# A 2-D recurrent scan on one core: the last output stage on four quadrants, and two fetches of `seq` later in the queue

## The chip, the cores and the metric

The kernel runs on one core of a Trainium2 chip. The metric is device time in microseconds (us) of one execution, median of three runs. Names of the engines: PE multiplies matrices (PEld is its weight load), DVE and ACT work on vectors, POOL on vectors too, SP only issues transfers here. PSUM is the memory that PE writes (the `bank`s), SBUF the one with 128 lanes that all engines read; DMA engines move data between SBUF and the chip's DRAM.

## The reference

`x` is (8 images, 192 channels, 128, 128) in fp32. It is group-normed (32 groups), then scanned by one GRU of 64 states in four directions (along the rows and the columns, forward and backward, same weights), each scan's states are projected back to 192 channels, and the mean of the four is added to `x`:

```
def _scan_direction(x, Wi, bi, W_ih, W_hh, b_ih, b_hh, Wo, bo, transpose, reverse):
    xs = jnp.transpose(x, (0, 3, 2, 1)) if transpose else jnp.transpose(x, (0, 2, 3, 1))
    if reverse:
        xs = xs[:, :, ::-1, :]
    seq = xs.reshape(b * A, T, c) @ Wi.T + bi
    hs = _gru_scan(seq, W_ih, W_hh, b_ih, b_hh)      # r, z, n gates, 128 steps
    out = hs @ Wo.T + bo
    ...
return x + (right + down + left + up) / 4.0          # of the group-normed x
```

## The kernel before

Images go in pairs: lanes 0 to 63 hold one image's 64 values, lanes 64 to 127 (`HIGH`; the others are `LOW`) the other's. There are four pairs, `g` = 0 to 3. For a pair, `seq` (128 lanes x 16384 pixels) holds the projected input of the GRU and `hsum` the sum of the states of all directions. A pair's **scan** has 128 steps `t`; each step does two chains, `c` = 0 (rows) and 1 (columns), 256 positions each, both directions in one. So the four scans are 4 x 128 steps one after the other.

Beside the scan of pair `g` other work is woven into its steps, by tables that are computed at the top:

- the **next pair's input**: x of pair g + 1 comes in 32 tiles of 512 pixels (m = 0 to 31) through three slots `xp`, is projected by PE (`project_high`, `project_straight`, `project_crossed`), gets its bias on ACT into `stage`, and goes out to DRAM as `seq_next`, two tiles at a time (`store_seq`). `project_at` gives the step at which a tile's first matmuls run (71 + 7m // 4), `project_ends` the step of its last ones. `x_next_at` asks for a tile's x four steps before.
- **`seq` is refilled while the scan still reads it.** A scan reads pixels from both ends and turns at the middle, so squares of `seq` become free one after the other. `fetch_seq(g, k)` brings square k = 0, 1, 2 (2 MB, 2.4 MB, 1.3 MB) from `seq_next` to `seq`; before, at step `grown_at[k] + 4` = 99, 115, 123. It waits on SP until `seq_next`'s tiles of this square have landed (`stage_stored`). The borders follow by `fetch_border`.
- the **last pair's output**: 96 units (a third of a tile each) of pair g - 1 are multiplied by `Wo` on PE in quadrants of 64 x 64, `hsum` coming back from DRAM and x again into `xf`; these tiles already lie in the form "k c", 3 blocks of 64 channels on 64 lanes.

All of these transfers are issued by SP, in the order of one loop over the steps. SP takes one after the other: while it waits for a semaphore at one of them, nothing behind it is issued.

The last pair has no scan after it, so its output is the stage called **End** (`finish_last` on PE and DVE, `load_last` on SP, `store_last` on ACT): 32 tiles of 512 pixels, for each three banks of (128 lanes x 512). A tile of x, 0.786 MB, is loaded to one of 14 slots `xe`, `Wo`'s product is added to it in place, and it is stored from the same slot. Tile i >= 14 can be loaded only once tile i - 14 has been stored. Slots 0 to 13 are loaded in the last scan's steps, as their memory (`xp`, blocks of `seq`, `xf`) comes free. The banks are used in two sets of three, so PE starts tile i when DVE has finished tile i - 2. In the form before, blocks 0 and 1 of a slot hold channels 0 to 127 of image one and two, on 128 lanes, and block 2 the other 64 channels of both images:

```
def finish_last():                       # PE, before
    for k, wo in enumerate((wo_a, wo_b, wo_c)):
        for side in range(2):
            last = pe.matmul(natural(fin_ps[s][k][:, :], side), wo[:, :],
                             columns(hsum[:, :, rows_of(i), :], side), ...)
```

## Time and profile before

| | us |
|---|---|
| median of 3 runs | 2526.6 (2522.61 to 2531.65) |
| the profiled execution | 2523.95 |
| its span | 2522.2 |
| statistics and first projection, up to the first step | some 200 |
| four scans, up to 2406.6 | some 2200 |
| End, from 2406.6 | 115.6 |

| engine | busy us | share of the span |
|---|---|---|
| PE | 2199.8 | 87% |
| DVE | 2035.9 | 81% |
| ACT | 1621.5 | 64% |
| POOL | 1533.2 | 61% |

How to read it: the shares are of the whole span, and each stretch has a limit of its own. The granted clock of PE was 0.987 of full speed over the span. In the page's 40 slices the DMA engines are busy 9 tenths of the time at the start, in the later halves of the scans of pairs 0 to 2, and in the last two slices. Times in the rows are from the start of the span. The time from a transfer's issue to its landing is in the views too.

### The profile page before, as it was taken

Reading aid. Unit: us, or ns where it says so; the run is one execution under the profiler, and the core shown is the slowest. Engines: PE = TensorE matmul, PEld = TensorE weight load, DVE = VectorE, ACT = ScalarE, POOL = GpSimd, SP = SyncE. Lnnn points to the kernel's source line nnn. Section 1 sums busy time; section 2 is a strip of 40 time slices with the busy share of each in tenths; the row PEclk is TensorE's granted clock in tenths of the full one; section 3 lists DMA queues with packets and bytes.
Section 4 is the critical chain, followed back from the end, with each engine's and each line's share of the span. In section 5 each row is a group of like instructions: output and inputs, shape, how many; then the busy total and the mean of one; then the engine's idle time right before and its main releaser. Section 6 shows DMA issues by size and latency. Waiting matters only on the chain.

```text
span 2522.2 us, 80883 instructions
## 1 busy us (share of the span) xinstructions
PE 2199.8 (87%) x31528; PEld 1444.4 (57%) x31528; DVE 2035.9 (81%) x4883; ACT 1621.5 (64%) x3401; POOL 1533.2 (61%) x2114
## 2 busy tenths in 40 slices
PE   0679999899979999899979999899979999999995
PEld 0345555566546666566656666566656677555574
DVE  7229999777769999787879999888867777888874
ACT  0236666677758887676758788677657888666600
POOL 2016666667766666566766666667666677666610
PEclk9999999999999999999999999999999999999998
DMA  9983332347789997589999998589986655333699
GB/s 355 288 219 96 96 96 67 85 141 218 230 241 244 240 246 177 153 224 260 308 267 250 233 246 207 142 221 263 313 258 165 152 146 129 73 94 94 154 322 363
DMA packets 325723, 509.25 MB, mean 202 GB/s; under 512 B 24928, under 2 KB 140000, under 8 KB 325344
## 3 DMA queue, kind: packets, MB, share of 16 engines
q1 hardware_dynamic: 307296, 478.23, 69.0%
q10 hardware_dynamic: 18048, 25.85, 2.9%
q8 instruction: 252, 4.13, 0.7%
q14 instruction: 127, 1.04, 0.1%
HBM read 352.98 MB, written 151.01 MB: 200 GB/s over the span
## 4 chain that ended last, share of the span: by engine, by line
PE 34%; DVE 22%; ACT 22%; issue 11%; DMA 6%; POOL 3%; SPq 1%; ACTq 0%; POOLq 0%; DVEq 0%
PE bank L855 19%; DVE r L994 8%; ACT bank L663 8%; ACT r L655 7%; ACT z L659 7%; DVE h L1008 5%; DMA work<-x 4%; DVE bank L999 4%; PE bank L856 4%; PE bank L835 3%; DVE r L989 2%; PE bank L837 2%; PE bank L953 2%; POOL hsum L529 1%; DVE bn L1119 1%
## 5 line engine op out<-in xcount | busy, mean ns | idle before, releaser
L855 PE MATMUL bank<-h,wh 64*64 64x256 f32 x6144 | 1515.0, 384 | 121.2 <-DVE h L1008 120.6
L835 PE MATMUL bank<-seq,wx 64*64 64x256 f32 x6144 | 1551.3, 385 | 62.7 <-DMA seq<-seq_next 24.0
L837 PE MATMUL bank<-seq,wx 64*64 64x256 f32 x6144 | 1551.9, 385 | 0.0
L856 PE MATMUL bank<-h,wh 64*64 64x256 f32 x6144 | 1523.9, 386 | 0.3 <-issue 0.3
L537 POOL TENSOR_TENSOR v<-z,h 128x256 f32<-128x256 f32 x1024 | 746.9, 730 | 778.7 <-ACT z L659 777.6
L855 PEld LDWEIGHTS bank<-h,wh 64*64 64x64 f32 x6144 | 727.4, 132 | 483.6 <-PE bank L837 336.6
L835 PEld LDWEIGHTS bank<-seq,wx 64*64 64x64 f32 x6144 | 741.7, 132 | 355.9 <-DVE r L994 208.2
L545 POOL TENSOR_TENSOR hsum<-hsum,h 128x256 f32<-128x256 f32 x1024 | 752.0, 734 | 94.1 <-DVE h L1008 65.1
L837 PEld LDWEIGHTS bank<-seq,wx 64*64 64x64 f32 x6144 | 740.0, 132 | 16.7 <-issue 1.2
L856 PEld LDWEIGHTS bank<-h,wh 64*64 64x64 f32 x6144 | 730.3, 132 | 1.2 <-issue 0.7
L989 DVE SCALAR_TENSOR_TENSOR r<-bank,bhh,r 128x256 f32<-128x256 f32 x1024 | 491.0, 479 | 296.0 <-ACT r L655 242.3
L659 ACT ACTIVATE z<-bank,brz 128x256 f32<-128x256 f32 x1024 | 486.5, 475 | 313.0 <-PE bank L856 300.1
L655 ACT ACTIVATE r<-bank,brz 128x256 f32<-128x256 f32 x1024 | 486.6, 475 | 211.9 <-PE bank L856 200.9
L663 ACT ACTIVATE bank<-r,bih 128x256 f32<-128x256 f32 x1024 | 488.3, 477 | 85.8 <-DVE r L994 59.4
L999 DVE SCALAR_TENSOR_TENSOR bank<-z,bank 128x256 f32<-128x256 f32 x1024 | 434.2, 424 | 74.9 <-ACT bank L663 71.2
L994 DVE TENSOR_TENSOR r<-bank,r 128x256 f32<-128x256 f32 x1024 | 431.2, 421 | 17.6
L1008 DVE TENSOR_TENSOR h<-v,bank 128x256 f32<-128x256 f32 x1024 | 425.5, 416 | 22.3 <-POOL v L537 1.6
L981 DVE BATCH_NORM_STATS2 bn<-work 128x6 f32<-128x384 f32 x384 | 212.4, 553 | 4.0 <-DMA work<-x 4.0
L819 PE MATMUL bank<-work,wo_a 64*64 64x256 f32 x768 | 202.6, 381 | 1.3 <-issue 1.3
L803 PE MATMUL bank<-work,ident 64*64 64x256 f32 x756 | 203.0, 389 | 0.0
L821 PE MATMUL bank<-work,wo_b 64*64 64x256 f32 x768 | 202.2, 381 | 0.0
L801 PE MATMUL bank<-work,ident 64*64 64x256 f32 x756 | 197.5, 381 | 0.8 <-DMA work<-x 0.8
(95 smaller groups left out, 2446.6 us busy)
## 6 DMA issues: line engine op xcount, KB each, us to landing
work<-x SPq DMA_DIRECT2D x384, 384.0 KB, 6.2
out<-work SPq DMA_DIRECT2D x192, 384.0 KB, 4.7
work<-x SPq DMA_DIRECT2D x143, 512.0 KB, 7.1
work<-x SPq DMA_DIRECT2D x286, 128.0 KB, 7.1
work<-x SPq DMA_DIRECT2D x32, 768.0 KB, 6.5
seq_next<-work SPq DMA_DIRECT2D x48, 512.0 KB, 6.3
work<-hsum_last SPq DMA_DIRECT2D x48, 512.0 KB, 6.5
seq<-x SPq DMA_DIRECT2D x17, 512.0 KB, 7.6
```

The costliest lines, as they stand in the source:

```text
L537: pool.tensor_tensor(v[:, c, :], z[:, c, :], h[:, c, (t + 1) % 2, :], ALU.mult).then_inc(v_ready[c], 1)
L545: pool.tensor_tensor(px, px, as_pair(h[:, c, t % 2, :], c), ALU.add).then_inc(h_added[c], 1)
L655: act.activation(r[:, c, :], rx_ps[c][:, 0:N2], ACT.Sigmoid, bias=brz[:, 0:1]).then_inc(r_ready[c], 1)
L659: act.activation(z[:, c, :], z_ps[c][:, 0:N2], ACT.Sigmoid, bias=brz[:, 1:2]).then_inc(z_ready[c], 1)
L663: act.activation(hn_ps[c][:, 0:N2], r[:, c, :], ACT.Tanh, bias=bih[:, 2:3]).then_inc(n_ready[c], 1)
L835: pe.matmul(as_pair(ps[LOW, :], c), wx[HIGH, gate, :], px[HIGH], start=start, stop=False, skip_group_check=True)
L837: return pe.matmul(as_pair(ps[HIGH, :], c), wx[LOW, gate, :], px[LOW], start=start, stop=False, skip_group_check=True)
L855: pe.matmul(ps[LOW, 0:N2], wh[LOW, gate, :], state[LOW], start=start, stop=True, skip_group_check=True)
L856: return pe.matmul(ps[HIGH, 0:N2], wh[HIGH, gate, :], state[HIGH], start=start, stop=True, skip_group_check=True)
L989: dve.scalar_tensor_tensor(out=r[:, c, :], in0=hn_ps[c][:, 0:N2], scalar=bhh[:, 2:3], in1=r[:, c, :], op0=ALU.add, op1=ALU.mult).then_inc( ...
L994: dve.tensor_tensor(r[:, c, :], rx_ps[c][:, N2:2 * N2], r[:, c, :], ALU.add).then_inc(t2_ready[c], 1)
L1008: dve.tensor_tensor(h[:, c, t % 2, :], v[:, c, :], hn_ps[c][:, N2:2 * N2], ALU.subtract)\
```

## The change

Two things are changed.

**End.** The product with `Wo` goes by quadrants of 64 x 64 in place of 128 x 128: 12 matmuls a tile and not 6, in pairs that read `LOW` and `HIGH` lanes. Each image's 192 channels now lie as three blocks of 64 channels: image a has blocks 0 and 2 on its own half of the lanes and block 1 on the other half (`last_parts`). So a tile is loaded and stored by 4 transfers, each on 64 lanes (two of 256 KB, two of 128 KB), where there were 3 (512 KB on 128 lanes, two of 128 KB on 64). Bytes and the 2 KB runs stay. Semaphores count to 64 and not 48. DVE's three additions a tile stay, with other bias columns; the load of `bo_low` at the start is gone.

**The squares of `seq`.** Square k is asked for at the later of `grown_at[k] + 4` and four steps behind the end of its last projected tile (tiles 15, 23, 27 end at steps 98, 112, 119). Square 0 goes from step 99 to 102, square 1 from 115 to 116, square 2 stays at 123.

```diff
     PRO = SPART // XW
-    N_WEIGHT_LOADS = 6 + 2 * (7 + 3 * 4)
+    N_WEIGHT_LOADS = 5 + 2 * (7 + 3 * 4)
     WSLOTS = 9
...
     dump_at = {grown_at[k] + 2: k for k in range(3)}
-    fetch_at = {grown_at[k] + 4: k for k in range(3)}
+    last_tile = [2 * (TILES // 2 - SQUARES[k] // (2 * ROWS)) - 1 for k in range(3)]
+    fetch_at = {}
+    for k in range(3):
+        ends = next(t for t, m in project_ends.items() if m == last_tile[k])
+        fetch_at[max(grown_at[k] + 4, ends + 4)] = k
...
         bi2 = sb("bi2", [P, 1])
-        bo_low = sb("bo_low", [P, 1])
         bo_high = sb("bo_high", [P, 1])
...
+        def last_parts(a):
+            return (((LOW, HIGH)[a], slice(0, 3, 2)), ((HIGH, LOW)[a], slice(1, 2)))
         def unit_bias(u):
...
                 if i >= TSLOTS:
-                    sp.wait_ge(xe_stored[s], 48 * (i // TSLOTS))
+                    sp.wait_ge(xe_stored[s], 64 * (i // TSLOTS))
                 elif s < XPS:
...
                     sp.wait_ge(xf_stored[k], 32 * ((TILES * (PAIRS - 1) + XFS - 1 - k) // XFS))
-                load_x(xe[s], PAIRS - 1, i, xe_loaded[s])
+                px = slice(i * TILE, (i + 1) * TILE)
+                for a in range(2):
+                    src = x_px[2 * (PAIRS - 1) + a, :, px].rearrange("(k c) n -> c k n", k=3)
+                    for lanes, blocks in last_parts(a):
+                        sp.dma_start(xe[s][lanes, blocks, :], src[:, blocks, :]).then_inc(xe_loaded[s], 16)
...
             load(s_hb[:, :], sel_high_b)
-            load(bo_low[:, :], bo_col[0:CLOW, :])
             for k in range(2):
...
                 px = slice(i * TILE, (i + 1) * TILE)
-                images = slice(2 * (PAIRS - 1), 2 * PAIRS)
-                act.dma_start(out_px[images, 0:CLOW, px].rearrange("b c n -> c b n"), xe[s][:, 0:2, :])\
-                   .then_inc(xe_stored[s], 16)
-                for k in range(2):
-                    act.dma_start(out_px[2 * (PAIRS - 1) + k, CLOW:C, px], xe[s][k * D:(k + 1) * D, 2, :])\
-                       .then_inc(xe_stored[s], 16)
+                for a in range(2):
+                    dst = out_px[2 * (PAIRS - 1) + a, :, px].rearrange("(k c) n -> c k n", k=3)
+                    for lanes, blocks in last_parts(a):
+                        act.dma_start(dst[:, blocks, :], xe[s][lanes, blocks, :]).then_inc(xe_stored[s], 16)
...
             for s in range(TSLOTS):
-                act.wait_ge(xe_stored[s], 48 * ((TILES + TSLOTS - 1 - s) // TSLOTS))
+                act.wait_ge(xe_stored[s], 64 * ((TILES + TSLOTS - 1 - s) // TSLOTS))
...
                         pe.wait_ge(x_finished, i - 1)
-                    for k, wo in enumerate((wo_a, wo_b, wo_c)):
-                        for side in range(2):
-                            last = pe.matmul(natural(fin_ps[s][k][:, :], side), wo[:, :],
-                                             columns(hsum[:, :, rows_of(i), :], side), start=side == 0, stop=True,
+                    for side in range(2):
+                        px = columns(hsum[:, :, rows_of(i), :], side)
+                        for k, low, high, low_out in ((0, wo_a[LOW, LOW], wo_b[HIGH, LOW], LOW),
+                                                      (1, wo_a[LOW, HIGH], wo_b[HIGH, HIGH], HIGH),
+                                                      (2, wo_c[LOW, LOW], wo_c[HIGH, HIGH], LOW)):
+                            ps = fin_ps[s][k]
+                            high_out = HIGH if low_out == LOW else LOW
+                            pe.matmul(natural(ps[low_out], side), low, px[LOW], start=side == 0, stop=True,
+                                      skip_group_check=True)
+                            last = pe.matmul(natural(ps[high_out], side), high, px[HIGH], start=side == 0, stop=True,
                                              skip_group_check=True)
...
                     dve.wait_ge(fin_ready, i + 1)
-                    dve.wait_ge(xe_loaded[s], 48 * (i // TSLOTS + 1))
+                    dve.wait_ge(xe_loaded[s], 64 * (i // TSLOTS + 1))
                     for k in range(3):
...
                             out=xe[s][:, k, :], in0=fin_ps[i % 2][k][:, :],
-                            scalar=(bo_low if k < 2 else bo_high)[:, 0:1], in1=xe[s][:, k, :],
+                            scalar=unit_bias(k), in1=xe[s][:, k, :],
                             op0=ALU.add, op1=ALU.add)
...
```

On SP, in the scan of pair 1 at steps 98 to 102. L350 and L352 load a tile of x for the projection (m = 18 and 19 are the first two here), L379 is `store_seq`, L389 `fetch_seq` of square 0, L424, L446 and L434 are the sums, the stores and the x of the output units. Before:

```order
L350 DMA work<-x 128x2x512 [waits xp_used]
L352 DMA work<-x 64x512 x2
L379 DMA seq_next<-work 1024x1x128 [waits staged]
L389 DMA seq<-seq_next 128x4x1024 [waits stage_stored0,stage_stored1,x_z_ready1,x_z_ready0]
L350 DMA work<-x 128x2x512 [waits xp_used]
L352 DMA work<-x 64x512 x2
L424 DMA work<-hsum_last 128x8x128 [waits unit_ready]
L446 DMA out<-work 64x3x512 [waits unit_finished,unit_added]
L446 DMA out<-work 64x3x512
L434 DMA work<-x 64x3x512 [waits xf_stored1]
```

The same place now (the lines have moved: L359 and L361 load x, L388 is `store_seq`, L398 the fetch, L433, L455 and L443 are the units'):

```order
L388 DMA seq_next<-work 1024x1x128 [waits staged]
L359 DMA work<-x 128x2x512 [waits xp_used]
L361 DMA work<-x 64x512 x2
L433 DMA work<-hsum_last 128x8x128 [waits unit_ready]
L455 DMA out<-work 64x3x512 [waits unit_finished,unit_added]
L455 DMA out<-work 64x3x512
L443 DMA work<-x 64x3x512 [waits xf_stored1]
L443 DMA work<-x 64x3x512
L359 DMA work<-x 128x2x512 [waits xp_used]
L361 DMA work<-x 64x512 x2
L388 DMA seq_next<-work 1024x1x128 [waits staged]
L398 DMA seq<-seq_next 128x4x1024 [waits stage_stored0,stage_stored1,x_z_ready1,x_z_ready0]
```

The fetch has moved behind the x of tiles 19 and 20, the sums, the stores and the x of the units, and one more `store_seq`; what stood behind it at step 100 now follows `store_seq` at once.

On PE, the first tile of End before (a row that ends in x2 is the two sides):

```order
L953 MATMUL bank0<-hsum,wo_a 128x4x64 [waits h_added1,h_added0]
L953 MATMUL bank0<-hsum,wo_a 128x4x64
L953 MATMUL bank1<-hsum,wo_b 128x4x64 x2
L953 MATMUL bank2<-hsum,wo_c 128x4x64 x2
L953 MATMUL bank3<-hsum,wo_a 128x4x64 x2
```

And now, one side of it and the beginning of the other (L968 reads `LOW` lanes, L970 `HIGH` ones):

```order
L968 MATMUL bank0<-hsum,wo_a 64x4x64 [waits h_added1,h_added0]
L970 MATMUL bank0<-hsum,wo_b 64x4x64
L968 MATMUL bank1<-hsum,wo_a 64x4x64
L970 MATMUL bank1<-hsum,wo_b 64x4x64
L968 MATMUL bank2<-hsum,wo_c 64x4x64
L970 MATMUL bank2<-hsum,wo_c 64x4x64
L968 MATMUL bank0<-hsum,wo_a 64x4x64
```

The three banks of one side now come first, then those of the other; bank 0 and bank 2 use the two quadrants on the diagonal, bank 1 the two off it.

## Rows read from the trace of the kernel before

**Rows 1.** Timeline of SP, pair 1, steps 97 to 103: start, us, what.

```profile
1162.28 0.57 SPq L379 DMA_DIRECT2D seq_next<-work  x1
1173.87 0.37 SPq L389 DMA_DIRECT2D seq<-seq_next  x1
```

**Rows 2.** Waits (us in total, times, longest) of PE, SP; last of PE, 1174 to 1210.

```profile
PE bank L706 <- DVE mv L1060: 79.2, 1, 79.2
...
SPq L387 <- DMA seq_next<-work: 24.8, 4, 10.9
...
PE bank L751 <- issue: 2.8, 1, 2.8
```

**Rows 3.** Timeline of DVE: the state h of chain 0, steps 93, 100, 107 (pair 1), 100, 107 (pair 2).

```profile
1139.59 0.41 DVE L1008 TENSOR_TENSOR h<-v,bank 128x256 f32<-128x256 f32 x1
...
1170.16 0.41 DVE L1008 TENSOR_TENSOR h<-v,bank 128x256 f32<-128x256 f32 x1
...
1204.98 0.41 DVE L1008 TENSOR_TENSOR h<-v,bank 128x256 f32<-128x256 f32 x1
...
1741.83 0.41 DVE L1008 TENSOR_TENSOR h<-v,bank 128x256 f32<-128x256 f32 x1
...
1773.16 0.41 DVE L1008 TENSOR_TENSOR h<-v,bank 128x256 f32<-128x256 f32 x1
```

**Rows 4.** Timeline of SP, pair 1, steps 114 to 119.

```profile
1236.04 1.69 SPq L389 DMA_DIRECT2D seq<-seq_next  x2
...
1246.56 0.90 SPq L379 DMA_DIRECT2D seq_next<-work  x1
```

**Rows 5.** Lines L352 (1253.5 to 1255.3; issue to landing) and L751 (1261 to 1267).

```profile
DMA to landing us min/median/max: 8.7/8.9/9.0
...
L751 PE MATMUL bank<-work,wc x4: 376/376/376, 1264.5 to 1265.2; 64*64 64x256 f32 x4
```

**Rows 6.** The chain that ended last, in order of time, from 2406.

```profile
2406.64 41.79 PE bank L953 x180
...
2489.88 8.18 DMA seq<-x
```

**Rows 7.** Stretches of End: busy us (instructions) of PE, PEld, DVE, ACT, POOL; clock, DMA share, GB/s.

```profile
2410.00:2420.00 10.00, 10.00 (x45) 8.40 (x44) 7.01 (x11) 0.00 (x0) 0.00 (x0) 0.95 0.95 288
2420.00:2430.00 10.00, 10.00 (x47) 8.44 (x46) 7.63 (x12) 0.00 (x0) 0.00 (x0) 1.00 1.01 354
```

**Rows 8.** DMA, 2440 to 2480, by queue (q10 ACT's, q1 SP's): packets, MB, share of 16 engines.

```profile
q10 hardware_dynamic: 4303, 7.83, 52.5%
q1 hardware_dynamic: 4323, 7.88, 52.2%
```

**Rows 9.** DMA, 2500 to 2518: End's last stores alone.

```profile
q10 hardware_dynamic: 3386, 6.18, 98.6%
```

**Rows 10.** DMA, 1923.5 to 1929 (two stores), then 1929 to 1935.5 (two loads), 64 lanes each.

```profile
q1 hardware_dynamic: 416, 0.79, 57.3%
...
q1 hardware_dynamic: 416, 0.79, 51.3%
```

**Rows 11.** DMA, 1949.5 to 1951.5: the first of two such stores alone.

```profile
q1 hardware_dynamic: 187, 0.38, 90.7%
```

**Rows 12.** Timeline of ACT's queue, 2506 to 2509: issues of stores.

```profile
2507.95 0.60 ACTq L685 DMA_DIRECT2D out<-work  x1
2508.58 0.52 ACTq L688 DMA_DIRECT2D out<-work  x1
```

**Rows 13.** Timeline of PE at 2388 (quadrants in the scan) and of DVE at 2427 (End).

```profile
2388.43 0.38 PE L856 MATMUL bank<-h,wh 64*64 64x256 f32 x1
2388.44 0.38 PE L835 MATMUL bank<-seq,wx 64*64 64x256 f32 x1
...
2388.65 0.38 PE L856 MATMUL bank<-h,wh 64*64 64x256 f32 x1
...
2427.18 1.41 DVE L1106 SCALAR_TENSOR_TENSOR seq<-bank,bo_low,seq 128x512 f32<-128x512 f32 x2 [0.59 <-PE bank L953]
```

## The prediction, made before the changed kernel had run

> **What bounds the kernel now.** I read SP's queue first, then the lengths of the steps, then End with its DMA queues. Nearly all of the span is the scan: one step follows the other, 4.4 us each (30.57 / 7, below), and its chain is not touched. So only two places can move: the steps that a fetch of `seq` disturbs, and End.
>
> *The fetch of square 0.* SP issues the store of `seq_next` at 1162.28 and the fetch only at 1173.87 [rows 1]: it waits for that store to land, 10.9 us at the longest and 24.8 in four such waits [rows 2]. Behind it stands the x of tile 19, issued right behind the fetch's 2 MB. PE then waits 2.8 us at L751, the first matmul of a projected tile [rows 2]. What the whole disturbance costs is best read from the steps, since the pattern of projected tiles repeats every seven of them: in pair 1, steps 93 to 100 take 1170.16 - 1139.59 = 30.57 us, steps 100 to 107 take 1204.98 - 1170.16 = 34.82; in pair 2, steps 100 to 107 take 1773.16 - 1741.83 = 31.33 [rows 3]. The excess is 4.25 and 0.8 us. In pair 0 no output units share the queue; I count nothing there.
>
> *End.* By the chain it is PE's at first: 41.79 us without a gap for 180 passes [rows 6], and a tile is 12 passes, so 2.8 us a tile (0.22 us a pass at full clock, 2.66 a tile). But the chain leaves PE at 2448 and ends behind a load and the last stores, and the DMA engines are full from 2420 on: share 1.01, and 0.95 already in the ten us before [rows 7]. A tile is 0.786 MB in and 0.786 MB out. I turn each row on DMA into the time that the 16 engines need for one such half, share x stretch x 0.786 / MB:
>
> - loads and stores together: (0.525 + 0.522) x 40 x 0.786 / 15.71 = 2.10 us [rows 8], so 4.2 us for a tile in and out;
> - stores alone, as they are now: 0.986 x 18 x 0.786 / 6.18 = 2.26 us [rows 9].
>
> 4.2 us is far over PE's 2.7. So End is bound by the transfers, in three parts: a head until the stores flow, some 18 tiles that go in and out (14 of 32 are loaded ahead), and a tail of stores alone. The tail begins where the last load has landed, 2489.88 + 8.18 = 2498.1 [rows 6], and lasts 24 us, that is 10 tiles at 2.26 and the last landing.
>
> **The change part by part.** The sum is made against the profiled execution, 2523.95 us (span 2522.2); it lies 2.6 us under the median of the runs, 2526.6, which I add at the end.
>
> *One weight load less.* Worth 0: at the start PE waits 79.2 us for DVE's statistics [rows 2], and the weights land in their shadow. If that cover were gone it would be worth one issue, 0.6 us.
>
> *Square 0 at step 102.* SP no longer waits there, since the store that it needs was issued three steps before; the waiting falls on nothing, and tile 19's x goes out up to 9 us sooner. Every byte still has to go through, but DMA has had nothing new to do between 1162.28 and 1173.87 [rows 1], so this is idle time that is used, not work put elsewhere. Next late would be tile 21, whose x now stands behind the fetch: at 4.37 us a step from 1170.16, the fetch goes out at about 1179, the x once tile 18 is used up, after step 103, at about 1186, and it is wanted at step 107, near 1199. 13 us are enough for what is left of the fetch and a tile. I take the full excess: **-4.3 -0.8 = -5.1 us**; a gain beyond it has no row, so the bounds are -5.1 and 0.
>
> *Square 1 at step 116.* Here SP hardly waited. The fetch moves from 1236.04 behind the stores, tile 28's x and the `store_seq` of 1246.56 [rows 4], 10 us later, ahead of tile 29's x. That tile has no room: its last two transfers are issued by 1255.3 and take up to 9.0 us, so it lands at about 1264, and PE begins it at 1264.5 [rows 5]. If DMA stays busy in between, the same bytes lie ahead of tile 29 and nothing moves; between 1236 and 1247 it has a dump of 2.4 MB, a tile, the stores and a `store_seq`, some 4.5 MB by the code's sizes, which is 11 us at 394 GB/s, so it stays nearly busy. I take 0, bounds -1 and +3 us in each of pairs 1 and 2.
>
> *End, PE.* Quadrants on both diagonals run at once in the scan: two products start at 2388.43 and 2388.44 on different quadrants, and the next at 2388.65, 0.22 us later [rows 13], as long as a pass of the full array takes. Eight of a tile's twelve products lie in the two diagonal quadrants, four in each, one behind the other, at two passes each: 8 x 0.22 = 1.75 us and not 2.66. If quadrants off the diagonal did not overlap, it would be 2.66 as now. DVE then sets the pace: its additions start every 0.66 us, two in 1.41 [rows 13], 2.0 us a tile. What it brings is only the head: 2410 to 2430 move 288 and 354 GB/s, 2.9 and 3.5 MB [rows 7] where 394 are possible [rows 8]: 1.06 + 0.4 = 1.46 MB, 3.7 us, would be the whole of it. But loads of the last slots fill half of that stretch, and the first store can come only some 1.2 us sooner. I take **-2 us**, bounds -4 and 0.
>
> *End, the transfers.* No byte is added, but all of it now goes by 64 lanes at a time, where it was one third. Two stores of 384 KB on 64 lanes each, one half behind the other, take 0.573 x 5.5 x 0.786 / 0.79 = 3.1 us [rows 10], against 2.26 in the tail; two such loads 0.513 x 6.5 x 0.786 / 0.79 = 3.3. While the first of the stores is alone, it is 0.907 x 2 x 0.786 / 0.38 = 3.75 us [rows 11]; so the rest of the pair, where both halves of the lanes overlap, goes at (3.15 - 1.81) x 0.786 / 0.41 = 2.6. 0.38 MB in 2 us is 190 GB/s.
> The Trainium skill says the same of this row ("SBUF — State Buffer", Door 1: The DMA port swizzle): lanes 0 to 63 reach 8 of the 16 ports, 218 GB/s at most by its table; and "DMA: Bandwidth & Descriptors", Rules for kernel authors, tells one not to split a transfer into halves of the lanes but to use one of 128. The row agrees with the first, and by both this part of the change costs time; what its rate would do to all of End is the second rival's case.
> In the tail one queue's stores follow each other, three blocks on the low half, three on the high half. That is the pair's case, with the lone start only once. I take the middle of 2.6 and 3.1, 2.85 us a tile, so **+6 us** for 10 tiles; bounds +3 and +9. Where loads and stores alternate I take no loss: there the third that goes by 64 lanes costs nothing now, 2.10 being the least of all stretches though stores alone need 2.26. That step I trust least.
> The fourth issue: ACT's take 0.60 and 0.52 us [rows 12], so four are 2.3 to 2.4 us a tile, under 2.85 and under 4.2. Worth 0; if the lanes cost nothing, it would be +1 us in the tail.
>
> **Sum:** -5.1 - 2 + 6 = -1.1 us, 2522.9 in the profiled execution; with the 2.6 us to the median, **2525 us**.
>
> **The rivals.**
>
> *The lanes cost little (chance 0.2).* The engines drift apart in a long stream, one half of them on the low lanes while the other is on the high ones, and the tail stays at 2.3 us: -5.1 - 3 + 1 = -7.1, 2519.5. For it: in [rows 8] a third of the bytes on 64 lanes leaves no mark. Against it: [rows 10, 11]. Half of this case, with a fuller head, is under -7.6.
>
> *The lanes bind while loads and stores alternate too (0.25): slower.* All loads now use half of the lanes at a time, and if a lane's way in and out is one and the same, or both queues fall on the same half together, a tile costs up to 3.1 + 3.3 = 6.4 us in place of 4.2. Over 18 tiles that is 40 us at the most; half of it, 20, is the value: 2525 + 20 = 2545. It decides as soon as a tile in and out needs over 4.7 us, 0.5 x 18 = 9 us. For it: single queues show the loss plainly [rows 10, 11]. Against it: the least time of all in [rows 8]. By the skill's 218 GB/s for one half, were both queues always on the same one, 1.57 MB would take 7.2 us, an estimate from that page.
>
> *Square 1's delay eats the gain (0.1).* Tile 29 lands 3 us later in pairs 1 and 2: +6, 2531.
>
> **How the numbers follow.** Forecast 0.45 at 2525, its own range 2520 to 2531; 0.2 at 2519.5; 0.25 at 2545 (2532 to 2566); 0.1 at 2531. A measurement tells some 0.3%, 7.6 us, from no change, so faster means under 2519 and slower over 2534.2. Faster: half of the second case and a little of the first, 0.12. Slower: most of the 0.25 and the ends of two others, 0.27. The same: 0.61. The range 2516 to 2545 leaves out half of the slow case and little below.
>
> **What would show it.** Steps 100 to 107 of pairs 1 and 2 at 30.4 to 30.6 us, and no wait of SP for `seq_next` of 10 us: the fetch's step is right. DVE's three additions starting every 0.66 us with no gap between tiles: PE's quadrants overlap. Tail stores at 2.85 us a tile and the mixed stretch at 4.2: the lanes' step is right; a share of 1 with fewer than 370 GB/s in the mixed stretch would make it wrong, as would a wait at tile 21 or 29.

## The result, and the profile after

| | before | after |
|---|---|---|
| median of 10 runs, us | 2524.56 (2513.65 to 2531.65) | 2538.49 (2526.89 to 2547.79) |
| the profiled execution, us | 2523.95 | 2526.89 |
| last state `h` of chain 0, from the span's start | 2404.2 | 2400.4 |
| from there to the end | 118.0 | 124.7 |

The changed kernel is slower: its time is 1.0055 of that before, with a 95% interval of 1.0039 to 1.0071, 14 us by the medians. The prediction said 2525 us, no change that could be measured, and gave "within 0.3%" a chance of 0.61 and slower 0.27. The measured median lies in its range of 2516 to 2545, but beyond the 2520 to 2531 that it gave its own account.

The profiled execution of after happens to be the fastest of its ten runs. So medians carry every comparison of size here, and the traces say where in the program time went. In the two traces the scans end 3.8 us sooner and End lasts 6.7 us longer.

The page of the kernel after: the busy line, and the last two rows of the 40 slices (the DMA engines' share in tenths and GB/s).

```profile
PE 2183.3 (86%) x31912; PEld 1411.3 (56%) x31912; DVE 2034.0 (81%) x4883; ACT 1619.1 (64%) x3401; POOL 1531.2 (61%) x2114
...
DMA  9973332356788996689999996689986664333699
GB/s 363 295 214 96 95 95 72 90 145 207 250 242 231 246 237 170 175 232 288 293 265 239 240 238 172 179 227 282 294 223 157 152 149 123 71 95 95 153 329 346
```

**The fetches.** SP's timeline, pair 1, steps 97 to 103, to be held against [rows 1]. The fetch of square 0 (L398) follows the store of `seq_next` (L388) by 0.76 us, where it was 11.6 us.

```profile
1169.88 0.59 SPq L388 DMA_DIRECT2D seq_next<-work  x1
1170.64 0.79 SPq L398 DMA_DIRECT2D seq<-seq_next  x1
```

DVE's timeline, state `h` of chain 0 at steps 100, 107, 114, 121 of pair 1 and then of pair 2, as in [rows 3] (L1008 there is L1024 here).

```profile
1161.26 0.41 DVE L1024 TENSOR_TENSOR h<-v,bank 128x256 f32<-128x256 f32 x1
1191.68 0.41 DVE L1024 TENSOR_TENSOR h<-v,bank 128x256 f32<-128x256 f32 x1
1222.10 0.41 DVE L1024 TENSOR_TENSOR h<-v,bank 128x256 f32<-128x256 f32 x1
1256.23 0.41 DVE L1024 TENSOR_TENSOR h<-v,bank 128x256 f32<-128x256 f32 x1
...
1731.10 0.41 DVE L1024 TENSOR_TENSOR h<-v,bank 128x256 f32<-128x256 f32 x1
1761.90 0.41 DVE L1024 TENSOR_TENSOR h<-v,bank 128x256 f32<-128x256 f32 x1
1792.60 0.41 DVE L1024 TENSOR_TENSOR h<-v,bank 128x256 f32<-128x256 f32 x1
1827.20 0.41 DVE L1024 TENSOR_TENSOR h<-v,bank 128x256 f32<-128x256 f32 x1
```

The differences are the lengths of seven steps each. Undisturbed ones take 30.42 us. Steps 100 to 107 are clean now (30.42 and 30.80). Steps 114 to 121, which took 30.62 and 31.12 us before, take 34.13 and 34.60.

What stopped them is tile 29 of the next pair's input. In order: SP's timeline, pair 1 (L398 is the fetch of square 1, L359 and L361 the x of tile 29); the issue-to-landing time of L361's two transfers; PE's waits from 1225 to 1257; and PE in two stretches of 4 us and one of 2 (columns as in [rows 7]).

```profile
1234.21 2.36 SPq L398 DMA_DIRECT2D seq<-seq_next  x2
...
1237.97 0.61 SPq L359 DMA_DIRECT2D work<-x  x1
1238.62 2.72 SPq L361 DMA_DIRECT2D work<-x  x2
```

```profile
DMA to landing us min/median/max: 13.1/13.4/13.7
```

```profile
PE bank L761 <- issue: 2.9, 1, 2.9
```

```profile
1250.00:1254.00 4.00, 1.11 (x17) 0.51 (x16) 0.91 (x2) 1.84 (x5) 1.84 (x3) 0.94 1.07 254
1254.00:1258.00 4.00, 4.00 (x44) 2.90 (x48) 1.79 (x5) 0.84 (x2) 0.64 (x1) 0.63 1.08 344
...
1254.00:1256.00 2.00, 2.00 (x20) 1.39 (x24) 0.83 (x3) 0.00 (x0) 0.00 (x0) 0.50 1.05 339
```

The x is issued 3.8 us behind the fetch and takes up to 13.7 us to land, where it took 9.0 [rows 5]: the fetch's 2.4 MB and two loads of x for the output units lie right in front of it. It lands at 1240.74 + 13.07 = 1253.81, and PE starts the tile at 1253.90. PE waited 2.9 us, and then its granted clock was 0.63 over 4 us, 0.50 in the first two of them (the lower of its two levels, 1.2 GHz). The seven steps lost 3.7. Steps 121 to 127 are longer as well, 26.7 and 28.1 us in pairs 1 and 2 where before has 25.8 and 26.0.

In before, that x was issued 16.9 us behind the fetch (1236.04 in [rows 4]):

```profile
1252.90 0.60 SPq L350 DMA_DIRECT2D work<-x  x1
```

**End.** PE, DVE and DMA in stretches, columns as in [rows 7].

```profile
2410.00:2420.00 10.00, 9.23 (x118) 5.33 (x118) 9.74 (x16) 0.00 (x0) 0.00 (x0) 1.00 1.05 345
2420.00:2430.00 10.00, 9.62 (x120) 5.33 (x118) 9.66 (x16) 0.00 (x0) 0.00 (x0) 1.00 1.03 347
...
2440.00:2480.00 40.00, 26.25 (x276) 13.91 (x270) 22.09 (x33) 0.00 (x0) 0.00 (x0) 0.86 1.06 380
...
2503.00:2521.00 18.00, 0.00 (x0) 0.00 (x0) 0.00 (x0) 0.00 (x0) 0.00 (x0) 0.50 0.94 258
```

In the head DVE is now the busy engine (9.74 of 10 us, 16 additions) and not PE. Counted from the last `h`, the two stretches of 10 us move 345 and 347 GB/s, where before moves 287 and 384: sooner at work, but not faster for long. In the mixed stretch 380 GB/s move, where [rows 8] give (7.83 + 7.88) MB in 40 us = 393. In the tail it is 258, where [rows 9] give 343. The queues of the tail (q10 is ACT's), then ACT's timeline there, then the landing times of its stores:

```profile
q10 hardware_dynamic: 2653, 4.65, 93.8%
```

```profile
2502.27 10.36 ACTq L699 DMA_DIRECT2D out<-work  x14
```

```profile
DMA to landing us min/median/max: 3.0/3.5/3.6
```

By the sum's own formula the tail is 0.938 x 18 x 0.786 / 4.65 = 2.85 us of engine time a tile, just the number forecast; at 258 GB/s a tile takes 3.05 us of elapsed time. But ACT's line says more. Its 14 stores take 10.36 us with no gap: 0.74 us each, four to a tile, 2.96. ACT never stops issuing, and a store lands 3.0 to 3.6 us after it was issued. The same reading was there before, and the prediction had cut it short. Timeline of ACT in the kernel before:

```profile
2505.70 0.67 ACTq L685 DMA_DIRECT2D out<-work  x1
2506.39 1.52 ACTq L688 DMA_DIRECT2D out<-work  x2
2507.95 0.60 ACTq L685 DMA_DIRECT2D out<-work  x1
2508.58 1.56 ACTq L688 DMA_DIRECT2D out<-work  x2
```

Three issues fill the 2.25 us from one tile to the next there too.

### The profile page after: what moved, and what is told of

Its sections match the earlier page's. It is cut to its first block, busy times and chain, and to the rows that moved or that the text cites. A ratio compares the mean times of both kernels' runs of the same rounds, so it can differ in the third digit from the quotient of the medians.

```text
span 2525.1 us, 81714 instructions
## 1 busy us (share of the span) xinstructions
PE 2183.3 (86%) x31912; PEld 1411.3 (56%) x31912; DVE 2034.0 (81%) x4883; ACT 1619.1 (64%) x3401; POOL 1531.2 (61%) x2114
## 4 chain that ended last, share of the span: by engine, by line
PE 33%; DVE 22%; ACT 21%; issue 12%; DMA 5%; POOL 3%; ACTq 1%; SPq 1%; DVEq 0%; POOLq 0%
PE bank L865 19%; DVE r L1010 8%; ACT bank L675 8%; ACT r L667 6%; ACT z L671 6%; DVE h L1024 5%; DVE bank L1015 4%; PE bank L866 4%; DMA work<-x 4%; PE bank L845 4%; DVE r L1005 2%; PE bank L847 2%; POOL hsum L542 1%; ACTq L699 1%; DVE bn L1135 1%
## 5 line engine op out<-in xcount | busy, mean ns | idle before, releaser
L1024 DVE TENSOR_TENSOR h<-v,bank 128x256 f32<-128x256 f32 x1024 | 424.9, 415 | 22.4 <-POOL v L550 1.6
```

The costliest lines, as they stand in the source:

```text
L1024: dve.tensor_tensor(h[:, c, t % 2, :], v[:, c, :], hn_ps[c][:, N2:2 * N2], ALU.subtract)\
```

## The experiments

Medians are of 4 to 12 runs; each ratio is against the kernel before on the same chip, with its 95% interval. "End" is the time from the last state `h` of chain 0 to the end of the span in the profiled execution, 118.0 before and 124.7 after. It varies from one execution to the next, and some runs below show by how much, as their code of End is the same: 118.0, 117.2, 116.4 and 118.6 us in before, fetch_only, square0 and square1_late, but 124.7 and 131.2 in after and end_only.

### The two parts apart

**fetch_only**: only the new `fetch_at`, squares 0, 1, 2 at steps 102, 116, 123.

> The kernel before with the later fetches alone: square 0 at step 102, square 1 at 116; End is that of before. Theory 1 (square 0's gain is paid back at tile 29): seven steps 100 to 107 at 30.4 us in pairs 1 and 2, seven steps 114 to 121 at 34.1 to 34.6 in place of 30.6 and 31.1, so -5 + 7 = +2 us against the kernel before, within 0.3% of it, and nearly all of the slow-down of the changed kernel is End's. Rival (the fetches cost the most): as slow as the changed kernel, +10 us or more.

2528.21 us, 1.0005 [0.9984, 1.0027]: no difference.

**end_only**: only End, as in the diff of the change.

> The kernel before with the changed End alone: quadrants on PE, all transfers on 64 lanes, fetches as before. Theory 1: End takes some 125 us from the end of the scan where it took 118, all of it in the tail of stores (3.0 us a tile for 2.3) and a little where loads and stores alternate (380 GB/s for 394); +7 to +12 us. Rival: End is not the place, 0 to +3 us.

2540.43 us, 1.0061 [1.0037, 1.0085]. End is 131.2 us. So End alone costs 16 us by the medians (13 in the traces) where the sum had +4, and the fetches give nothing where it had -5.1. Each of the two had its error.

**square0**: the first square moved, nothing else.

```diff
-    fetch_at = {grown_at[k] + 4: k for k in range(3)}
+    fetch_at = {grown_at[0] + 7: 0, grown_at[1] + 4: 1, grown_at[2] + 4: 2}
```

> The kernel before with square 0 fetched at step 102, square 1 at 115 as before, End as before. Theory 1: steps 100 to 107 at 30.4 us in both pairs, steps 114 to 121 at 30.6 to 31.1, -5 us, 0.2%. Rival (the gain comes back anyway, since DMA has the same bytes to move): steps 107 to 121 longer by what 100 to 107 gained, 0 us.

2517.36 us, 0.9974 [0.9959, 0.9990]. Steps 100 to 107 take 30.42 and 30.43 us, and 114 to 121 take 30.61 and 31.13. Square 0's step is right, and fetch_only's second half took its gain away. The eleven runs of this section whose fetches are as before show pair 2's steps 100 to 107 at 32.5 to 34.65 us, where [rows 3] had 31.33; so the 0.8 us for pair 2 was read from an execution at the low end of what varies.

**square1_late**: square 1 moved too, but to step 118, where its place in SP's queue is behind the x of tile 29.

```diff
-    fetch_at = {grown_at[k] + 4: k for k in range(3)}
+    fetch_at = {grown_at[0] + 7: 0, grown_at[1] + 7: 1, grown_at[2] + 4: 2}
```

> The kernel before with square 0 at step 102 and square 1 at 118, behind the x of tile 29 (asked for at 117) and not just ahead of it as at 116. Theory A (it is the place in the queue: whatever tile stands right behind a fetch is late, and tile 29 had no room, tile 30 has 7 us): steps 114 to 121 at 30.4 to 30.6 us in pairs 1 and 2, as fast as square0 or up to 1 us faster. Theory B (it is the delay itself: the fetch's bytes must go before tile 29 or 30 whatever the order): steps 114 to 121 or 121 to 127 again 3 to 4 us longer.

2518.47 us, 0.9964 [0.9948, 0.9980]. States `h` of chain 0 at steps 107, 114, 121 of pair 1:

```profile
1198.81 0.41 DVE L1008 TENSOR_TENSOR h<-v,bank 128x256 f32<-128x256 f32 x1
...
1230.48 0.41 DVE L1008 TENSOR_TENSOR h<-v,bank 128x256 f32<-128x256 f32 x1
...
1261.10 0.41 DVE L1008 TENSOR_TENSOR h<-v,bank 128x256 f32<-128x256 f32 x1
```

Steps 114 to 121 take 30.62 us in both pairs, in fetch_only 35.0 and 33.55, and steps 121 to 127 are as before. (Steps 107 to 114 took 31.67 us here, 30.42 elsewhere; the fetch of square 1 comes after them, and what held them is not known.) SP issues the x of tile 29 at 1244.51 and the fetch at 1246.61. The fetch at step 118 costs nothing that shows, the one at 116 the whole gain. So it is not the delay that hurts but what the fetch stands in front of.

### Which part of End costs the time

**lanes_only**: the transfers by halves of the lanes, PE's product as before. To keep the old layout a 256 KB transfer takes 64 channels of both images.

```diff
+        last_parts = ((LOW, slice(0, 2)), (HIGH, slice(2, 3)), (HIGH, slice(0, 2)), (LOW, slice(2, 3)))
...
+                for lanes, blocks in last_parts:
+                    if blocks == slice(0, 2):
+                        dst = out_px[both, lanes, px].rearrange("b c n -> c b n")
...
+                    act.dma_start(dst, xe[s][lanes, blocks, :]).then_inc(xe_stored[s], 16)
```

> The kernel before with PE, DVE and the placing of the channels of before, but each tile of End loaded and stored by four transfers of 64 lanes, in the order low 2 blocks, high 1, high 2, low 1, as in the changed kernel. Theory 1 (the lanes cost the time): the tail at 2.9 to 3.0 us a tile, and End even 2 to 3 us longer than in end_only, since PE's head start is missing: +9 to +14 us. Rival (the quadrants on PE or the runs of DVE cost it): as the kernel before, 0 to +2 us, tail at 2.3 us a tile.

2542.25 us, 1.0066 [1.0045, 1.0088], End 131.8: as long as end_only, so the transfers cost what End loses.

**quadrants_only**: the twelve products on quadrants, transfers as before.

```diff
-                    for k, wo in enumerate((wo_a, wo_b, wo_c)):
-                        for side in range(2):
...
+                    for side in range(2):
+                        px = columns(hsum[:, :, rows_of(i), :], side)
+                        for k, out, wo, of in ((0, LOW, wo_a[LOW, LOW], LOW), (1, HIGH, wo_b[HIGH, HIGH], HIGH),
+                                               (0, HIGH, wo_a[LOW, HIGH], LOW), (1, LOW, wo_b[HIGH, LOW], HIGH),
+                                               (2, LOW, wo_c[LOW, LOW], LOW), (2, HIGH, wo_c[HIGH, HIGH], HIGH)):
```

> The kernel before with End's products in quadrants of 64 x 64, but the layout and all transfers of before: fin_ps[0] from the low lanes to both halves, fin_ps[1] from the high ones. Theory 1 (End is bound by the transfers, the quadrants only start it sooner): tiles ready every 2.0 us for 2.66, first store 1 us sooner, End 116 to 117 us for 117.9, tail at 2.3 us a tile: -1 us, no difference that can be measured. Rival (the quadrants on PE are what slows End): +5 us or more. Rival 2 (PE's pace was a bound): -5 us or more.

2523.2 us, 0.9994 [0.9976, 1.0012]. Its head in stretches of 10 us:

```profile
2401.80:2411.80 10.00, 9.39 (x120) 5.62 (x116) 9.27 (x14) 0.00 (x0) 0.00 (x0) 1.00 1.03 317
2411.80:2421.80 10.00, 9.39 (x116) 5.06 (x116) 9.72 (x16) 0.00 (x0) 0.00 (x0) 1.00 1.04 387
```

The same two stretches behind the last `h` move 280 and 337 GB/s in before. End is 113.2 us in the trace, and 113.3 in that of best (below), where the four with the old End had 116.4 to 118.6. So the traces speak for some 4 us, the upper end of what the sum allowed; in the medians 1.5 us less can't be told from nothing.

**stores64** and **loads64**: of lanes_only, the stores alone (its lines above, with nothing done to SP's), and the loads alone:

```diff
-                load_x(xe[s], PAIRS - 1, i, xe_loaded[s])
+                for lanes, blocks in last_parts:
...
+                    sp.dma_start(xe[s][lanes, blocks, :], src).then_inc(xe_loaded[s], 16)
```

> lanes_only with the loads as before (3 transfers, 512 KB of a tile on 128 lanes); only the stores go by 64 lanes. Theory A (a queue's own packets meet on one half, loads and stores each for themselves): the tail as in lanes_only, 2.9 to 3.1 us a tile (+7 us), and about half of lanes_only's loss where loads and stores alternate. Rival (what alternates costs only where both queues are on 64 lanes): the alternating stretch as before, 4.0 us a tile.

2538.84 us, 1.0063 [1.0046, 1.0080], End 135.2.

> lanes_only with the stores as before; only the loads go by 64 lanes. Theory A: tail at 2.3 us a tile as before, no loss there; the last store 2 to 4 us later by the slower first loads and the other half of the loss where loads and stores alternate. Rival: as the kernel before, within 1 us.

2525.3 us, 1.0007 [0.9986, 1.0028], End 119.0. So the stores alone bring the whole loss. The same 64-lane shapes cost End nothing when they are loads, though the last load then lands 108 us behind the last `h` and not 94: the stores go on beside it.

**end_interleaved**: the four transfers in the order low, high, low, high, and not low, high, high, low.

```diff
+        interleaved = [(0, last_parts(0)[0]), (1, last_parts(1)[0]), (1, last_parts(1)[1]), (0, last_parts(0)[1])]
```

> end_only, with the four transfers of a tile in the order low 2 blocks, high 2, low 1, high 1, so that no more than 2 blocks in a row lie on one half of the lanes, where it was 3. Theory A (the engines meet on one half only as long as one queue's run of blocks lasts, so shorter runs overlap better): tail at 2.5 to 2.7 us a tile for 3.1, End 3 to 5 us shorter than end_only's 131. Theory B (the fourth issue on ACT sets the tail's pace, 4 x 0.7 us, whatever the order): tail as in end_only, 2.9 to 3.1 us a tile.

2545.9 us, 1.0071 [1.0047, 1.0094], End 132.9. The order of the halves does nothing that can be measured.

### Lanes or issues

**four_issues**: as before, but the 128-lane transfer cut in two, all four with the old lanes.

```diff
-                act.dma_start(out_px[images, 0:CLOW, px].rearrange("b c n -> c b n"), xe[s][:, 0:2, :])\
+                for k in range(2):
+                    act.dma_start(out_px[2 * (PAIRS - 1) + k, 0:CLOW, px], xe[s][:, k, :]).then_inc(xe_stored[s], 16)
```

> The kernel before with End's tiles moved by four transfers, two of 256 KB on all 128 lanes and the two of 128 KB on 64 lanes: one issue more, the lanes as before. Theory A (the lanes set the tail's pace): tail at 2.3 us a tile as before, End 117 to 119 us, no difference. Theory B (the fourth issue does, ACT's take 0.63 to 0.9 us each in the slow tail): tail at 2.9 to 3.1 us a tile and End some 7 us longer.

2525.83 us, 1.0018 [1.0004, 1.0033], End 117.9. Its issues take 0.57 us on the mean, so four of them with their gaps are 2.4 us. A fourth issue as such is free, or nearly (the interval just excludes 1).

**two_issues**: as end_only, but each image lies wholly on its own half, so a tile is two transfers of 384 KB on 64 lanes.

```diff
-                    for lanes, blocks in last_parts(a):
-                        act.dma_start(dst[:, blocks, :], xe[s][lanes, blocks, :]).then_inc(xe_stored[s], 16)
+                    act.dma_start(dst, xe[s][(LOW, HIGH)[a]]).then_inc(xe_stored[s], 16)
```

> Each image on its own half of the lanes, three blocks of 64 channels: two transfers a tile of 64 lanes x 3 blocks, 384 KB each, like those of the output units in the scan; PE goes by the two quadrants on the diagonal, two products at a time. Theory A (lanes): the run of three blocks on one half is as in the changed kernel, so the tail is at 2.9 to 3.1 us a tile and End at 128 to 132 us. Theory B (issues): two issues take 1.5 us, so the tail is bound by DMA at 2.3 us and End takes some 118 us.

2528.3 us, 1.0003 [0.9987, 1.0019], End 117.0. Stretches from its tail, and issue to landing there:

```profile
2510.00:2522.00 12.00, 0.00 (x0) 0.00 (x0) 1.88 (x3) 0.00 (x0) 0.00 (x0) 0.50 1.05 405
2522.00:2530.00 8.00, 0.00 (x0) 0.00 (x0) 0.00 (x0) 0.00 (x0) 0.00 (x0) 0.50 0.98 308
```

```profile
DMA to landing us min/median/max: 5.1/7.4/9.2
```

This is the run that breaks the lanes' step. Every byte goes by 64 lanes, first one half and then the other, on one queue; and the stores alone move 405 GB/s, 1.94 us a tile, more than the tail of before. What differs from after is that stores wait in the queue: they land 7.4 us after issue and not 3.5, and once that backlog is used up the rate falls to 308. The backlog is from the mixed stretch, where stores land after 15.8 us. It isn't kept up in the tail: nine issues take 12.95 us there, 2.9 us a tile, while a tile moves in 1.94.
The Trainium skill says of such transfers that "they serialize" ("DMA: Bandwidth & Descriptors", Rules for kernel authors), and gives one half at most 218 GB/s ("SBUF — State Buffer", Door 1: The DMA port swizzle). The second agrees with the lone store of [rows 11], 190 GB/s. The first does not hold for a stream that is queued: 405 GB/s here.

**split_four** and **split_three**: the layout of two_issues, with each image's store cut in two, and with only the second image's cut in two. The store of split_four, and the one line in which split_three differs from it:

```diff
+        end_parts = ((0, slice(0, 2)), (0, slice(2, 3)), (1, slice(0, 2)), (1, slice(2, 3)))
...
-                    act.dma_start(dst, xe[s][(LOW, HIGH)[a]]).then_inc(xe_stored[s], 16)
+                    act.dma_start(dst[:, blocks, :], xe[s][(LOW, HIGH)[a], blocks, :]).then_inc(xe_stored[s], 16)
```

```diff
-        end_parts = ((0, slice(0, 2)), (0, slice(2, 3)), (1, slice(0, 2)), (1, slice(2, 3)))
+        end_parts = ((0, slice(0, 3)), (1, slice(0, 2)), (1, slice(2, 3)))
```

> two_issues, with each image's transfer of 64 lanes x 3 blocks cut in 2 blocks and 1 block: same lanes, same layout, same products, the same run of three blocks on each half; four issues a tile in place of two. Theory B (in the tail ACT's issues set the pace, some 0.85 + 0.63 + 0.81 + 0.63 us, and the queue runs empty): tail at 2.9 to 3.1 us a tile, End 128 to 132 us, +10 to +14 us. Theory A (it is the changed kernel's lanes or its crossed placing, not the issues): tail at 1.9 to 2.0 us a tile as in two_issues, End 117 us.

2545.62 us, 1.0065 [1.0039, 1.0090], End 135.4.

> two_issues with the second image's transfer cut in 2 blocks and 1 block: three issues a tile, all on 64 lanes. Theory B (issues): they take 0.6 + 0.85 + 0.63, 2.1 to 2.3 us a tile, about what DMA takes; tail 2.1 to 2.4 us, End 117 to 120 us. Theory A (lanes, once the queue has little waiting): 2.6 to 3.0 us a tile.

2535.3 us, 1.0044 [1.0021, 1.0067], End 121.9. In stretches, split_three (mixed, and two pieces of the tail) and then split_four (mixed, tail):

```profile
2446.00:2486.00 40.00, 40.00 (x368) 26.72 (x365) 31.03 (x46) 0.00 (x0) 0.00 (x0) 1.00 1.05 404
2501.00:2511.00 10.00, 0.00 (x0) 0.00 (x0) 1.53 (x3) 0.00 (x0) 0.00 (x0) 0.50 1.04 378
2512.00:2526.00 14.00, 0.00 (x0) 0.00 (x0) 0.00 (x0) 0.00 (x0) 0.00 (x0) 0.50 0.97 247
```

```profile
2446.00:2486.00 40.00, 38.84 (x356) 29.14 (x354) 29.60 (x44) 0.00 (x0) 0.00 (x0) 1.00 1.03 360
2520.00:2538.00 18.00, 0.00 (x0) 0.00 (x0) 0.00 (x0) 0.00 (x0) 0.00 (x0) 0.50 0.96 253
```

The bytes, the lanes and the layout are those of two_issues in both. With two issues a tile the backlog lasts nearly to the end, with three it is gone for the last five tiles, with four there is hardly any, and then a tile takes 3.0 to 3.2 us. End is 117.0, 121.9 and 135.4 us for two, three and four issues, and the medians have the same order.

All of End's variants side by side. "Mixed" is a stretch of 40 us while loads and stores go together, "tail" one of 18 us of stores alone (two_issues: 12 us, split_three: 14). Landings are medians of ACT's stores from 40 to 80 us behind the last `h` and from 24 to 6 us before the end; the issue times are means of the latter.

| kernel | stores a tile: KB, lanes | mixed GB/s | landing | tail GB/s | landing | one issue | End us |
|---|---|---|---|---|---|---|---|
| before | 512 on 128, 2 x 128 on 64 | 396 | 8.4 | 343 | 3.4 | 0.73 | 118.0 |
| four_issues | 2 x 256 on 128, 2 x 128 on 64 | 395 | 6.0 | 328 | 3.0 | 0.57 | 117.9 |
| two_issues | 2 x 384 on 64 | 404 | 15.8 | 405 | 6.6 | 1.39 | 117.0 |
| split_three | 384, 256, 128, all on 64 | 404 | 10.8 | 247 | 4.1 | 1.01 | 121.9 |
| after | 2 x 256, 2 x 128, all on 64 | 380 | 7.6 | 258 | 3.4 | 0.73 | 124.7 |
| end_only | the same | 359 | 5.7 | 250 | 3.3 | 0.75 | 131.2 |
| lanes_only | the same, images mixed | 362 | 5.6 | 257 | 3.2 | 0.74 | 131.8 |
| stores64 | the same, loads as before | 353 | 5.6 | 252 | 3.3 | 0.74 | 135.2 |
| split_four | the same, an image on one half | 360 | 5.3 | 253 | 3.3 | 0.74 | 135.4 |

ACT spends 93% or more of both stretches issuing, in every row: it hardly ever lacks a tile. What goes with the rate is how much waits in the queue. With all on 64 lanes and landings at 3.3 to 4.1 us the tail moves 247 to 258 GB/s, which is the isolated pair's 3.1 us a tile [rows 10]; with landings at 7 us it moves 405. With 128 lanes in it, a short queue still moves 328 to 343. The mixed stretch has the same order: 353 to 362 GB/s at 5.3 to 5.7 us, 380 at 7.6, 404 above 10. four_issues, 395 at 6.0 us, has two thirds of its bytes on 128 lanes.

The trace of after shows both rates with one and the same code, 40 us each, and the landing times of ACT's stores in them:

```profile
2420.00:2460.00 40.00, 33.05 (x384) 18.07 (x382) 31.18 (x47) 0.00 (x0) 0.00 (x0) 0.94 1.05 355
2460.00:2500.00 40.00, 20.58 (x204) 10.56 (x198) 20.68 (x30) 0.00 (x0) 0.00 (x0) 0.84 1.06 402
```

```profile
DMA to landing us min/median/max: 5.1/5.6/7.6
...
DMA to landing us min/median/max: 3.9/10.0/14.4
```

The lanes and the four issues are the same in both; the backlog is not. end_only moves 349 to 372 GB/s in each 10 us from 2430 to 2490, and its End is 6.5 us longer. What lets the backlog grow in one execution and not in the other is not shown.

The table also says what the number of issues does not set. In the tail a tile's issues with their gaps take 2.3 us (three) and 2.4 (four) where some go by 128 lanes, and 2.9 to 3.1 where all go by 64, be they two, three or four. So in the tail ACT's pace goes with the lanes. What the number of 64-lane issues changes is how large the backlog gets before and how long it lasts.

### More queues

**end_two_queues**: of end_only's last 14 tiles, SP issues half of the stores.

```diff
+            for i in range(TILES - TSLOTS, TILES):
+                s = i % TSLOTS
+                sp.wait_ge(x_finished, i + 1)
+                px = slice(i * TILE, (i + 1) * TILE)
+                for a in (1, 0):
+                    dst = out_px[2 * (PAIRS - 1) + a, :, px].rearrange("(k c) n -> c k n", k=3)
+                    lanes, blocks = last_parts(a)[1]
+                    sp.dma_start(dst[:, blocks, :], xe[s][lanes, blocks, :]).then_inc(xe_stored[s], 16)
...
-                    for lanes, blocks in last_parts(a):
+                    for lanes, blocks in last_parts(a)[0:2 if i < TILES - TSLOTS else 1]:
```

> end_only, but for the last 14 tiles SP issues the two transfers of one block (low, then high), ACT those of two blocks (low, then high): two issues a queue and tile, both queues on the same half in the same order. Theory B (issues): tail at 1.9 to 2.3 us a tile in place of 3.1, End some 9 us shorter than end_only's 131. Theory A (lanes): 2.8 us and more, as both queues meet on the same half.

2533.25 us, 1.0035 [1.0016, 1.0055], End 121.9. Stretches at the start of its last stores and 12 us later:

```profile
2500.00:2510.00 10.00, 1.97 (x24) 0.95 (x20) 4.13 (x6) 0.00 (x0) 0.00 (x0) 0.84 1.06 405
...
2512.00:2524.00 12.00, 0.00 (x0) 0.00 (x0) 0.00 (x0) 0.00 (x0) 0.00 (x0) 0.50 1.02 342
```

The transfers are those of end_only, and 342 to 405 GB/s are back in place of 250: End gets 9 of its 13 us back. So the lanes of the single transfers do not hold the stream at 250; a second engine that issues lifts it. Whether that is by more work in the queues, or because two queues are more often on different halves of the lanes, this run doesn't tell.

**best**: squares at steps 102 and 118, the quadrants, transfers on 128 lanes as before. Its edit is the diffs of square1_late and of quadrants_only together.

> quadrants_only and square1_late together: square 0 at 102, square 1 at 118, quadrants on PE, transfers as before. The sum of the parts: -7 -1 = -8 us, 0.3% under the kernel before. If the parts take the gain from each other, as square0 alone or less.

2513.14 us (2508.81 to 2518.06), 0.9954 [0.9936, 0.9971]: faster than both kernels. End is 113.3 us. Its gain over before is shown; its gain over square1_late (0.9964) is not.

**best_two_queues**: best, with SP taking the 128 KB stores of the last 14 tiles.

```diff
+            for i in range(TILES - TSLOTS, TILES):
...
+                for k in range(2):
+                    sp.dma_start(out_px[2 * (PAIRS - 1) + k, CLOW:C, px], xe[s][k * D:(k + 1) * D, 2, :])\
+                      .then_inc(xe_stored[s], 16)
```

> best (squares 0 and 1 later, quadrants on PE, transfers on 128 lanes), with the two small stores of each of the last 14 tiles issued by SP, which has nothing to do there. Theory B: ACT's three issues hold the tail of best at 2.0 to 2.3 us a tile; with one on ACT and two on SP it falls to 1.95, some 2 us less than best, so 0.5% under the kernel before. Rival: DMA is at its end anyway, no difference from best.

2515.22 us, 0.9949 [0.9930, 0.9969], End 114.9: no difference from best. In its trace 2496 to 2504 move 403 GB/s, in that of best 2494 to 2502 move 317, so the second queue does raise the rate for a time; but End isn't shorter, and the 2 us that were expected are less than End varies by.

## Why the prediction was wrong, by its own steps

- *The weight load.* 0; not tested by itself.
- *Square 0, -5.1 us.* Right in place and mechanism: steps 100 to 107 at 30.42 and 30.80 us, the fetch 0.76 us behind the store; square0 alone gives 0.9974, 6.8 us. Bounded at -5.1 because no row showed more, it was sized a little low: pair 2's excess was read from one execution that had it at 0.8 us, and the others have 2 to 4. The text took DMA to have had nothing to do from 1162 to 1174; its share was 1.03 until 1170, 0.40 from 1170 to 1174 and 0.71 to 1178, so only the last part of the wait was idle time to be used.
- *Square 1, 0 with bounds of +3 in each pair.* **Wrong, and the first step that failed.** Measured +3.5 us in steps 114 to 121 of pairs 1 and 2 in after, +4.4 and +2.4 in fetch_only, against the 30.62 and 31.12 of before, and 0.8 to 2.1 more in steps 121 to 127. It was the third rival, with chance 0.1, and its sign, a wait at tile 29, came. The argument was that DMA is nearly busy anyhow, so that "the same bytes lie ahead of tile 29". They don't. The fetch had been issued 16.9 us ahead of tile 29's x (1236.04 and 1252.90 in the trace of before); now it is 3.8 us, and the x lands after 13.7 us and not 9.0. The text itself had found that tile without room, and a tile without room was reason enough to take the bound.
- *PE, -2 us.* The mechanism is right: in the head DVE sets the pace and the stores flow sooner. The traces with the old transfers give some 4 us, the medians don't settle it (quadrants_only 0.9994 [0.9976, 1.0012]), and in after it is lost in what follows.
- *The tail, +6 us.* **Sized too low.** 2.85 us of engine time a tile came out, but that was taken for the pace, which is 3.05 to 3.14 us at 258 to 250 GB/s. From the last load's landing to the end it is 24.1 us in before, 29.2 in after and 33.9 in end_only. So the profiled after fits the +6 only by luck, as it came to its tail with a backlog; end_only has +9.8, over the upper bound of +9. The reason given, that two halves on one queue overlap badly, holds while the queue is short and not when it is filled (two_issues, 405 GB/s). That is the rival by which "the engines drift apart" and the lanes cost little; the changed kernel does not keep its queue filled enough to get it.
- *The fourth issue, 0.* **Wrong, and with the lanes the step behind most of the loss.** It took 0.60 and 0.52 us from [rows 12] and made four of them 2.4 us a tile. A tile of before has a third issue, 1.0 us, and the three with their gaps already are the 2.26 us of the tail. [Rows 12] stopped one line short of showing that ACT is never idle there. On 64 lanes an issue is 0.74 us, and four are 3.05. It isn't the number of issues alone (four_issues: End 117.9) nor the lanes alone (two_issues: End 117.0), but the two together (split_four: 135.4), which the sum had added up as if each stood for itself.
- *The mixed stretch, 0, "that step I trust least".* It failed: 380 GB/s in after and 359 in end_only for 396. At 353 to 362 a tile in and out is 4.3 to 4.5 us where it was 4.0, 6 to 8 us over 17 tiles; the last load lands 97.3 us behind the last `h` in end_only and 93.9 in before, so 3.4 us of it are seen there. The second rival put this down to the lanes and wanted over 4.7 us a tile; it is much smaller, and not there when the same lanes are stored by two issues (404 GB/s). loads64 excludes the loads.

The sum, with what the runs give: square 0 at -7 and square 1 at +7 make fetch_only's 0; End is +16 by end_only. 0.05% and 0.61% make 0.66%, for 0.55% measured.

What stays open: why an issue lasts as long as it does. In the tail each begins 0.03 to 0.04 us after the last one's end and lasts 0.45 to 1.94 us; ACT may be the cause of the short queue, or be held by something that the profile doesn't show. In split_three, three issues take the 3.1 us that four take in split_four, so a fixed cost of an issue is excluded. In best_two_queues, at 403 to 406 GB/s, an issue of 512 KB lasts 2.4 us on ACT and one of 128 KB 1.1 to 1.2 on SP, so with a full queue an issue is at least in part a wait. That more issuing capacity helps is shown by end_two_queues; that more bytes in one issue do, by two_issues.

## What to carry to other kernels

Before a large transfer is moved in a FIFO queue, look for the transfer right behind its new place that has no slack, and put it behind that one. The streams of stores here went fast while something waited in their queue: read the issue-to-landing time and whether the issuing engine has gaps, and add up all issues of one tile before calling a tail bound by the DMA engines. When two changes each cost nothing by themselves, the run to make is the one that has both.

## What the runs showed of the hardware

- The DMA engines' busy share does not say that they are full. In tails of stores alone it was 0.94 at 258 GB/s, 0.99 at 343 and 1.05 at 405. The GB/s told them apart far better.
- Stores on two halves of the lanes, one after the other on one queue, reach 405 GB/s when stores wait in the queue, and 247 to 258 when landings are at 3 to 4 us. With two thirds of the bytes on 128 lanes it is 328 to 343 at the same landings.
- The wait of PE at tile 29 cost more than its length. After its 2.9 us the granted clock was 0.63 over 4 us (0.50, the lower level, in the first two), where it is 1.00 in undisturbed steps, and the seven steps lost 3.7 us.
